# Reordering a two-layer gated cross-attention kernel on one Trainium2 core: the second attention's start, its slots, and a bias sum on GpSimd

## What is computed

```python
x = x + tanh(g_xattn[0]) * L0_xattn(layernorm(x), ctx)     # 16 heads of 16, biases on q, k, v, out
x = x + tanh(g_ffn[0])   * L0_ffn(layernorm(x))            # 8 experts, top 2, a rotation by 3 matrix exponentials, a gate
x = x + tanh(g_xattn[1]) * L1_xattn(layernorm(x), ctx)     # 16 heads of 64, LoRA on q, k, v, out
x = x + tanh(g_ffn[1])   * L1_ffn(layernorm(x))            # a shared expert and 8 routed ones, top 2

# L1_xattn: 371 context tokens by the usual keys and values, the last 4 by keys and values of their own
out = attention(q, k, v) + attention(q, k_ipa, v_ipa)
return out @ Wo + bo + lora_o(out)
```

## Time and profile before

| what | value |
|---|---|
| three runs | 989.82, 978.87 and 988.82 us, median 988.82 us |
| the profiled execution, its own time | 985.29 us |
| span from its first to its last instruction | 983.5 us |
| mean granted TensorE clock | 0.945 of full speed |
| first attention (from the first unit to the last product) | 27 to 272 us |
| router and layer 0's experts | 272 to 463 us |
| norm, own tokens and prologue of the second attention | 463 to 505 us |
| second attention | 505 to 832 us |
| layer 1's experts | 832 to 983 us |

### The profile page before, as it was taken

The page is one execution under the profiler, slowest core; times in us unless marked ns, Lnnn a source line. Parts: engine busy times, 40 slices in busy tenths (PEclk is TensorE's granted clock), DMA queues, the critical chain, the costliest instruction groups (busy, mean ns, idle before and its releaser), DMA issues.

```text
span 983.5 us, 21996 instructions
## 1 busy us (share of the span) xinstructions
PE 861.8 (88%) x7463; PEld 682.4 (69%) x7463; DVE 668.6 (68%) x1532; ACT 497.5 (51%) x1058; POOL 500.8 (51%) x525
## 2 busy tenths in 40 slices
PE   1789999999897999977679899898998976999994
PEld 1579988888775877755456677676776766666663
DVE  6487766666875768776657677777787777743333
ACT  4365555555533645542356655656556553334441
POOL 4779999998512324211126745556455562124420
PEclk9899999999856999998799999999999998999997
DMA  5423333347382225447002222222221248911114
GB/s 174 158 87 95 107 113 107 116 149 240 124 293 78 65 81 156 136 124 262 29 23 87 66 66 87 66 86 74 76 86 63 66 139 270 351 39 55 59 45 129
DMA packets 81485, 113.73 MB, mean 116 GB/s; under 512 B 7786, under 2 KB 60083, under 8 KB 81284
## 3 DMA queue, kind: packets, MB, share of 16 engines
q1 hardware_dynamic: 75556, 99.92, 32.0%
q0 software_dynamic: 4032, 11.02, 3.7%
q10 hardware_dynamic: 1824, 1.84, 0.5%
HBM read 75.78 MB, written 36.96 MB: 115 GB/s over the span
## 4 chain that ended last, share of the span: by engine, by line
PE 51%; DVE 15%; POOL 13%; issue 8%; ACT 6%; DMA 6%; SPq 0%; ACTq 0%; DVEq 0%; POOLq 0%
PE sp L892 5%; PE tp L906 5%; PE pb L850 5%; POOL Z L1296 4%; PE sp L2053 4%; PE tp L2053 3%; POOL Z L1304 3%; PE pb L2083 3%; POOL qz L1373 3%; PE tp L2278 3%; PE pb L871 3%; PE pb L844 3%; PE sp L1909 2%; ACT ST L1041 2%; PE pb L1927 2%
## 5 line engine op out<-in xcount | busy, mean ns | idle before, releaser
L1048 ACT ACTIVATE ST<-tp 125x672 f32<-125x672 f32 (+1 forms) x128 | 93.4, 730 | 156.3 <-PE tp L906 156.3
L892 PE MATMUL sp<-KT,qz 128*112 128x375 f16 (+1 forms) x768 | 118.5, 333 | 32.7 <-ACT ST L1041 21.2
L1296 POOL TENSOR_SCALAR Z<-Z 128x512 f32<-128x512 f32 x94 | 140.9, 1499 | 4.4 <-DMA Z<-in_moe 4.2
L906 PEld LDWEIGHTS tp<-identf,ST 112*125 112x125 f32 x768 | 98.5, 191 | 24.2 <-issue 14.3
L906 PE MATMUL tp<-identf,ST 112*125 112x112 f32 x768 | 111.6, 282 | 4.3 <-POOL ST L1404 3.3
L1304 POOL TENSOR_TENSOR Z<-Z 128x512 f16<-128x512 f32 x94 | 111.0, 1181 | 6.2
L892 PEld LDWEIGHTS sp<-KT,qz 128*112 128x112 f16 (+1 forms) x768 | 66.9, 129 | 63.7 <-ACT ST L1041 29.5
L1857 POOL DMA_INDIRECT back<-ST,slot_row x42 | 43.6, 1039 | 127.8 <-ACT ST L1967 67.1
L1851 POOL DMA_INDIRECT ST<-rows,slot_from x42 | 41.5, 988 | 93.6 <-DVE slot_weight L1836 52.7
L1177 DVE TENSOR_SCALAR_CACHE_REDUCE ST<-sp 112x375 f32<-112x375 f32 x128 | 65.0, 545 | 35.2 <-PE sp L892 35.1
L1404 POOL TENSOR_TENSOR ST<-pn,sums 112x8 f32<-112x8 f32 x64 | 12.9, 201 | 142.6 <-ACT ST L1041 142.6
(11 more groups left out here) (352 smaller groups left out, 1993.1 us busy)
## 6 DMA issues: line engine op xcount, KB each, us to landing
Z<-in_moe SPq DMA_DIRECT2D x86, 256.0 KB, 3.1
cut_scratch<-Z SPq DMA_DIRECT2D x86, 256.0 KB, 2.6
KT<-cut_scratch SPq DMA_DIRECT2D x16, 384.0 KB, 7.8
W<-cut_scratch SPq DMA_DIRECT2D x8, 512.0 KB, 5.6
W<-cut_scratch SPq DMA_DIRECT2D x32, 128.0 KB
W<-w_scratch SPq DMA_DIRECT2D x6, 512.0 KB, 8.8
V<-cut_scratch SPq DMA_DIRECT2D x8, 384.0 KB
own_scratch<-Z SPq DMA_DIRECT2D x8, 256.0 KB, 3.6
```

The source lines that it names most:

```text
L892: mm = pe.matmul(SB_[j][0:S, 0:L.keys], q, kT[bs % 2][qb][r, t, 0:L.keys], start=(n == 0), stop=(n == 2))
L906: mm = pe.transpose(TB_[j][0:CHUNK, c * S:(c + 1) * S], P_[:, st % 2, j, c * CHUNK:(c + 1) * CHUNK], identf[0:S, 0:S])
L1048: act.activation(PT[:, st % 2, :, 0, :] if l else PT0[:, st % 2, :, :], TP2[0:CHUNK, :, 0:NCH * S], ACT.Copy)\
L1296: pool.tensor_scalar(whole, whole, WS, None, ALU.mult).then_inc(s["cut_up"], 1)
```

## The change

It has seven parts. None changes what is computed.

1. **Slots.** Layer 1's front units move: q1 from slot 2 to 1, each k unit one slot ahead, i from 11 to 10. The value units keep theirs.
2. **Bias sum.** Layer 0's `out_bias_gpsimd` moves from the head of POOL's attention to behind `masks(1)`, in front of the third piece. SP issues the bias rows behind three more chunks.
3. **The expert bias.** Its transpose moves on PE in front of the last `abel` product.
4. **DVE before the experts.** `expm_first_vector` goes ahead of `bias_vector`, and `cut_x0_vector(0)` from behind `eyes_vector` to ahead of `expm_rest_vector`.
5. **Turning ahead of five keys.** In the second attention PE, ACT and DVE turn Y after three key units; DVE takes `turn_vector(3)` directly behind the norm, ahead of `ipa_vector` and of the cuts of k0 to k2, which no longer stand inside the norm. k3 to k7 move into the prologue.
6. **A new prologue order:** k0 k1 k2, q0 q1, k3 k4 k5, v0, k6 k7, then `scores(0)`, i, v1 to v5. The maxima and exponentials of pair 0 stand beside i, and no longer in batch 0.
7. **Waits.** q0 and q1 no longer wait for a free bank; v0 waits for q1; k3 to k7 wait for the cut of the key three before.

```diff
-            at = dict(enumerate((0, 2, 3, 4, 5, 6, 7, 8, 9, 10, 11, 12, 13, 13, 14, 15, 15)))
+            at = dict(enumerate((0, 1, 2, 3, 4, 5, 6, 7, 8, 9, 10, 12, 13, 13, 14, 15, 15)))
...
+        def first_order(L):
+            if L.index == 0:
+                return L.front
+            return L.k_units[:3] + L.q_units + L.k_units[3:6] + L.v_units[:1] + L.k_units[6:] + L.i_units + L.v_units[1:]
...
-            for _, kind, u, n, ns, _ in prologue_units(L):
-                if l and u == L.v_units[0]:
-                    pe.wait_ge(s["routed_in"][0], 16 * len(HOMES0) * E + 32)
-                unit(kind, u, n, ns, 0, 0)
-            scores(0, 0, 0)
+            if l == 0:
...
+            else:
+                for _, kind, u, n, ns, _ in prologue_units(L):
+                    if u[0] == "i":
+                        pe.wait_ge(s["ipa_lo"], 3)
+                        scores(0, 0, 0)
+                    if u == L.v_units[0]:
+                        pe.wait_ge(s["routed_in"][0], 16 * len(HOMES0) * E + 32)
+                    if u[0] == "k":
+                        ahead_tensor(pe, u[1])
+                    else:
+                        unit(kind, u, n, ns, 0, 0, free={L.q_units[0]: 0, L.q_units[1]: 0,
+                                                         L.v_units[0]: front_done(L, 0, 0, "q")}.get(u))
...
             for _, kind, u, n, ns, nh in prologue_units(L):
-                unit(kind, u, n, ns, 0, 0)
                 if u[0] == "i":
+                    for j in range(2):
+                        exps(0, 0, 0, j)
                     ipa_exp(0, 0)
+                elif u[0] == "k" and l:
+                    ahead_scalar(act, u[1])
...
             for _, kind, u, n, ns, nh in prologue_units(L):
+                if u[0] == "k" and l:
+                    ahead_vector(dve, u[1])
+                    continue
+                if u[0] == "i":
+                    maxima(0, 0, 0)
                 unit(kind, u, n, ns, nh, 0, 0)
...
-                out_bias_gpsimd(pool, 0)
                 masks(0, 0)
...
                             masks(b + 1, b + 1)
+                            if b == 0:
+                                out_bias_gpsimd(pool, 0)
...
             if n >= 3:
-                pe.wait_ge(s["g_free1"], n - 2)
+                pe.wait_ge(s["g_free1"], ahead_number(n - 3) + 1)
...
+                if b == B - 1:
+                    bias_turn_tensor(pe)
...
         def tiles0_vector(dve):
-            cut_x0_vector(dve, 0)
...
+            sp.wait_ge(s["chunk_lo"], 1)
+            chunks_sync(sp, NE, NE + 3)
             for l in range(2):
                 o = ROW[f"bo{l}"][0]
                 sp.dma_start(out_bias[:, l, :], a["rows"][0, o:o + C].partition_broadcast(S)).then_inc(s["w1_in"], 16)
-            sp.wait_ge(s["chunk_lo"], 1)
-            chunks_sync(sp, NE, NE + 3)
...
             norm_scalar(act, 3)
-            for n in range(3, FIRST_K):
-                ahead_scalar(act, n)
             turn_scalar(act, 3)
...
+            expm_first_vector(dve)
             bias_vector(dve)
-            expm_first_vector(dve)
+            cut_x0_vector(dve, 0)
             expm_rest_vector(dve)
...
-            norm_vector(dve, 3, X, Y, (0, 3))
+            norm_vector(dve, 3, X, Y)
+            turn_vector(dve, 3)
             ipa_vector(dve)
-            for n in range(3, FIRST_K):
+            for n in range(3):
                 ahead_vector(dve, n)
-            turn_vector(dve, 3)
             dve.wait_ge(s["const_set"], 2)
-            dve.wait_ge(s["g_free1"], FIRST_K)
...
             ipa_tensor(pe)
-            for n in range(FIRST_K):
+            for n in range(3):
                 ahead_tensor(pe, n)
             turn_tensor(pe, 3, Y, halves_of(3))
             pe.wait_ge(s["ln_tlo"], TURN0[4])
             pe.wait_ge(s["w1_in"], 16 * 6)
-            pe.wait_ge(s["ipa_lo"], 3)
```

More of the change, by code:

```diff
@@ L757, in unit_numbers @@
             return found
+        def first_order(L):
+            if L.index == 0:
+                return L.front
+            return L.k_units[:3] + L.q_units + L.k_units[3:6] + L.v_units[:1] + L.k_units[6:] + L.i_units + L.v_units[1:]
         def prologue_units(L):
-            ahead = L.k_units if L.index else []
-            rest = L.q_units + L.v_units + L.i_units if L.index else L.front
             found, done = [], 0
-            for n, u in enumerate(ahead + rest):
-                if u not in ahead:
+            for n, u in enumerate(first_order(L)):
+                if n >= (3 if L.index else 0):
                     found.append((0, "front", u, n, n, done))
@@ L785, in front_done @@
             if isinstance(bs, int) and bs == 0:
-                ahead = len(L.k_units)
-                return last if L.index == 0 else {"q": ahead + len(L.q_units), "k": ahead + len(L.q_units),
-                                                  "v": ahead + len(L.q_units) + len(L.v_units), "i": len(L.front)}[which]
+                if L.index == 0:
+                    return last
+                units = {"q": L.q_units, "k": L.k_units, "i": L.i_units, "v": L.v_units}[which]
+                return first_order(L).index(units[-1]) + 1
             if bs == 1 and isinstance(bv, int):
@@ L821, in wo, with unit @@
                 return w0("Wo", q, t) if l == 0 else W1[:, q, 6144 + t * C:6144 + (t + 1) * C]
-            def unit(kind, u, n, ns, bv, bs, behind=1):
+            def unit(kind, u, n, ns, bv, bs, behind=1, free=None):
                 bank = GB[ns % 2]
-                if ns >= 2:
-                    pe.wait_ge(g_free, n - 1)
+                if free is None:
+                    free = n - 1
+                if ns >= 2 and not (isinstance(free, int) and free == 0):
+                    pe.wait_ge(g_free, free)
                 if u[0] == "q":
@@ L955, in batch @@
                         scores(bv + 1, bs + 1, 0)
-            for _, kind, u, n, ns, _ in prologue_units(L):
-                if l and u == L.v_units[0]:
-                    pe.wait_ge(s["routed_in"][0], 16 * len(HOMES0) * E + 32)
-                unit(kind, u, n, ns, 0, 0)
-            scores(0, 0, 0)
+            if l == 0:
+                for _, kind, u, n, ns, _ in prologue_units(L):
+                    unit(kind, u, n, ns, 0, 0)
+                scores(0, 0, 0)
+            else:
+                for _, kind, u, n, ns, _ in prologue_units(L):
+                    if u[0] == "i":
+                        pe.wait_ge(s["ipa_lo"], 3)
+                        scores(0, 0, 0)
+                    if u == L.v_units[0]:
[5 more added lines that the diff above has]
+                                                         L.v_units[0]: front_done(L, 0, 0, "q")}.get(u))
             batch("first", 0, 0)
@@ L1060, in batch @@
                     for j in range(2):
-                        exps(bv, bs, p, j)
+                        if p or l == 0 or where != "first":
+                            exps(bv, bs, p, j)
                         for hh, kind, u, n, ns, nh in todo:
@@ L1215, in batch @@
                 for p in range(NP):
-                    maxima(bv, bs, p)
+                    if p or l == 0 or where != "first":
+                        maxima(bv, bs, p)
                     if bs or p >= 1:
```

9 lines of the change are left out of this document (6 added, 3 removed).

## The result

The changed kernel takes 979.4 us (median of 20 runs, 966.9 to 986.3) against 988.5 us (978.9 to 996.0, 20 runs). The ratio is 0.9874, with a 95% interval of 0.9850 to 0.9899: 12.4 us faster, with a forecast of 12.7, and within the 2% that I had called no difference.

A forecast was written before the change was run, and what follows sets the result against it. PE, busy 861.8 of 983.5 us, was taken as the bound, so its waits counted. Terms +2.4 - 3.8 - 5.5 - 5.8 = -12.7 took the median 988.82 to 976.1, stated as 976, range 966 to 986.

The forecast's parts named there:

- Start and bias sum: Layer 0's first attention: start 1.8 us sooner, RW's cut held 4.2 us by the moved sum; net +2.4 us.
- the held cut costs only its own 4.2 us: Batch 0 of layer 0: POOL's moved sum delays DVE's RW cut, making DVE 4.2 us later, all on the chain.
- as today: Batch 0 of layer 0: DVE's W cut goes next, POOL's 2.49 us piece ending only after it; cut ends at 49.2.
- POOL's 6.5 us: First attention: POOL's 6.5 us of added work goes into its 5.2 us wait for query cuts; costed at nothing.
- The case of the rival: First attention: POOL's waits for queries don't take up the sum; +4.1 us, giving 980; chance 0.10.
- Ahead of the experts: Before layer 0's experts: scaling fills DVE's idle gap and the first rows' cut comes sooner; -3.8 us.
- The second attention's start: From the second layer norm into batch 1: Y turned sooner, q0 at 478.5 instead of 484.50; -5.5 us.
- moves with the rest: Second attention: POOL starts its pieces sooner, so its bias sum, which holds PE until 545.92, comes sooner too.
- starts sooner for nothing: Second attention: PE reaches batch 1 early but gains nothing; the 5.5 us are lost, giving 981.6; chance 0.10.
- its second reason: Second attention: PE, arriving early, runs more units at the slow pace, so the 5.5 us are lost.
- The slots: Second attention: 0.75 us gained in each of five middle batches, 2.0 in batch 1; together -5.8 us.
- what is gained is one key unit: Middle batches of the second attention: t0 starts as today with k3 behind it; gain 0.79 us less 0.05 each.

The follow-up runs named there:

- the sum in eight: Changed kernel with layer 0's bias sum, in its new place in batch 0, split into eight instructions of 112x256: 973.9 us, ratio 0.9832.
- the sum behind the wait: Changed kernel with layer 0's bias sum behind `masks(2)`, in batch 1 of the first attention: 980.9 us, ratio 0.9896.
- the next edit: Changed kernel with DVE cutting the second query unit behind the maxima of pair 1, no longer ahead of them: 969.8 us, ratio 0.9762.

## Why the prediction was right

The total was right: 12.7 forecast, 12.4 measured. Its terms were not all so.

- **Start and bias sum, +2.4.** Right in size (+2.9, 0.0 to 5.7, for the move alone). The start is 1.8 us shorter once the 0.5 us by which x arrives later is taken off, and RW's cut is held for 5.03 us in six profiles of seven, as worked out. The step that failed is that the held cut costs only its own 4.2 us. PE runs at half clock behind it, or already behind W's cut, which the working had let go "as today" and which took 1.98 to 2.25 us beside POOL's masks in four of the nine profiles with the sum moved. In the seven with the whole sum in batch 0 the first attention is 6 to 11 us longer, and the second batch's first scores come 1.6 to 7.0 us later than before, in none of the seven the 2 to 3 us forecast. The many runs show less of this than the profiles; at 8.5 us for each hundredth of the mean clock (an estimate from the 20 runs below) the 0.940 against 0.943 above is some 3 us by itself. So that the time came to +2.9 may be partly luck.
- **POOL's 6.5 us, nothing.** Held up where the sum stands in front of the long query wait: with the sum in eight, POOL's last store comes no later than with the sum at the head. The case of the rival, up to +4.1 without that cover, is the sum behind the wait: 7.06.
- **Ahead of the experts, -3.8.** 4.2 in the trace. The first rows' cut came as worked out. The Trainium skill ("SBUF — State Buffer", section "SBUF: two separate sides") has a warning on DMAs that GpSimd issues beside DVE's work, from which I had feared 0.4 us. The traces agree in direction: the first two gathers' instructions take 2.03 and 1.61 us in all ten profiles with the new order, and 1.19 and 0.95 in the four with the old. PE waits up to 1.64 us for the first rows in the ten, but the stretch stays at 39.6 to 40.2 us, since the rows' cut waits for ACT's high parts.
- **The second attention's start, -5.5.** Right up to the third scores (q0 -6.0 as forecast, third scores -4.8). Beside old slots it is worth 6.7 us by the last scores. The step that failed is that the rest "moves with the rest" and the slots' gain comes on top: beside new slots 0.5 us is left in the traces and 1.8 in the time. The rival "starts sooner for nothing" came near, and its second reason was the right one, slow pace in batch 0; PE waits for POOL's sum as long as before, 1.47 us.
- **The slots, -5.8.** Undersized with the old start (10.6 us in the traces, 11.0 in the time) and oversized with the new one (4.5 and 4.3). In the middle batches the step at fault is "what is gained is one key unit": PE's idle time goes from 2.56 to 1.45 us, so 1.1 is gained, not 0.75, since t0's wait of 0.69 went as well. That is 5.6 us in place of 3.8. Batch 1 gave the 2.0 forecast, once clocks are alike. With the new start batch 0 takes some 2.8 us of it back (67.9 against a mean of 70.7), which the sum had at nothing. The third scores wait longer, as said, which made the next edit visible.

Start and slots together were forecast at 11.3 us and brought 11.2, but neither is worth its own term, and they don't add: each takes from the other. That their sum came out is luck in part, and the match of the total shows less than it seems to.

## What to carry to other kernels

When two engines exclude each other, count the longest single instruction, not the work: beside eight short sums a cut took 1.23 us, beside one long sum 5.03, in the same place. When a hole is filled, look at once which wait stands behind it; here the best edit moved one DVE cut behind the maxima that PE was really waiting for, and by the ratios it brought nearly as much again (11 us, of which the traces show 6) as the whole change. Test two gains together and apart: here each was worth far less beside the other. And an added piece of work is hidden by a wait only if it stands in front of that wait.

## What had not been expected of the hardware

PE stayed at half clock for 27 us while it was busy for 26.30 of them. What it had done just before was wait 1.95 us in one place. In the eight profiles with the whole sum in batch 0 or 1, in each of which a DVE cut was held up, PE's longest wait in this stage is 1.87 to 3.64 us and half clock sums to 17 to 27 us. In the six others the longest wait is 1.29 to 1.73 us and half clock sums to 6.8. What makes the clock fall, or keeps it low for 27 us of nearly full work in one profile and 10 in another, is not shown.

The spread of the runs goes with the clock: over the 20 runs of the changed kernel the mean granted clock goes from 0.930 to 0.951 and the time from 986.3 to 966.9, with a correlation of -0.97, some 8.5 us for each hundredth. A profile of one execution therefore has to be compared stage by stage, at stages whose clocks are alike.
